# An adaptive-norm, RWKV and mixture-of-experts layer on one core: the shared expert inside the batches' pipeline, and rows that carry base and gate

## What is computed

```python
mod = silu(c) @ wmod                       # per batch: sa, ca, ga, sb, cb, gb (ga, gb kept at least 0.25 in size)
h = layernorm(x) * (1 + ca) + sa
h = ln(h) * g1 + b1
xm = mix(h)                                # this token, the one before, and half of the one before or after
k, v, r = exp(min(xm @ Wk.T, 60)), xm @ Wv.T, xm @ Wr.T
h = h + (sigmoid(r) * wkv(k, v)) @ Wo.T    # two scans over the tokens, and a division
h = ln(h) * g2 + b2
xm = mix2(h)
h = h + sigmoid(xm @ Fr.T) * (relu(xm @ Fk.T)**2 @ Fv.T)      # Fk is 512 x 128
x = x + ga * h
h = layernorm(x) * (1 + cb) + sb
e = argmax(h @ w_router.T)                 # one of 16 experts per token, s = sigmoid(its logit)
routed = (silu(s*h @ G_e) * (s*h @ U_e)) @ D_e                # 256 wide
shared = (silu(h @ w_gate.T) * (h @ w_up.T)) @ w_down.T       # 256 wide
out = x + gb * (shared + routed)
```

## Time and profile before

| | |
|---|---|
| median of three runs | 391.36 us |
| the profiled execution | 393.6 us |
| its span | 391.8 us |
| PE busy | 296.8 us (76%) |
| DVE busy | 244.0 us (62%) |
| ACT busy | 179.3 us (46%) |
| POOL busy | 187.6 us (48%) |
| mean granted PE clock | 0.858 |

### The profile page before, as it was taken

How to read it: one execution, slowest core, us unless ns; L and a number is a source line. 1 busy time by engine, 2 the same in 40 slices (tenths; PEclk the granted TensorE clock), 3 DMA queues, 4 the chain that set the end, 5 groups by cost and what they waited for, 6 DMA issues and landing times.

```text
span 391.8 us, 4364 instructions
## 1 busy us (share of the span) xinstructions
PE 296.8 (76%) x1140; PEld 171.7 (44%) x1140; DVE 244.0 (62%) x514; ACT 179.3 (46%) x436; POOL 187.6 (48%) x267
## 2 busy tenths in 40 slices
PE   4363667877668766877795586699989999999844
PEld 4223234334433534544453343334436666666532
DVE  5148596997989889789688342634335444444423
ACT  2541654947556666555372543222214444444300
POOL 4542726558678485656273534310003666666610
PEclk9956598996998888767889598699999999999955
DMA  6688000102011010010010100132002222222057
GB/s 182 175 241 321 28 0 4 51 0 60 22 47 35 0 54 29 0 41 21 0 49 8 41 14 14 50 97 49 0 1 56 75 75 82 71 77 71 4 155 274
DMA packets 28184, 25.22 MB, mean 64 GB/s; under 512 B 3682, under 2 KB 21734, under 8 KB 28160
## 3 DMA queue, kind: packets, MB, share of 16 engines
q1 hardware_dynamic: 24480, 18.57, 16.5%
q0 software_dynamic: 2528, 4.27, 3.4%
q10 hardware_dynamic: 1152, 2.10, 1.4%
HBM read 17.42 MB, written 8.49 MB: 66 GB/s over the span
## 4 chain that ended last, share of the span: by engine, by line
PE 30%; DVE 24%; POOL 21%; issue 13%; ACT 7%; DMA 3%; SPq 0%; POOLq 0%; DVEq 0%; ACTq 0%
PE bank L858 23%; POOL y_rows L423 11%; PE bank L862 5%; DVE work L524 4%; POOL sorted_rows L400 4%; POOL work L377 3%; ACT work L724 2%; DMA work<-y_rows 2%; DVE work L543 2%; DVE work L519 2%; DVE work L517 1%; DVE work L541 1%; PE bank L901 1%; POOL work L381 1%; DVE work L528 1%
## 5 line engine op out<-in xcount | busy, mean ns | idle before, releaser
L423 POOL DMA_INDIRECT y_rows<-work x47 | 46.2, 982 | 71.2 <-ACT work L838 41.9
L862 PE MATMUL bank<-ident,work 128*128 128x128 f32 x192 | 40.2, 362 | 52.9 <-ACT work L724 23.9
L862 PEld LDWEIGHTS bank<-ident,work 128*128 128x128 f32 x192 | 29.9, 185 | 75.0 <-ACT work L724 28.9
L858 PE MATMUL bank<-up_experts,work 128*128 x94 | 48.2, 595 | 0.0
L685 DVE COPY work<-bank 128x256 f32<-128x256 f32 x47 | 19.9, 424 | 37.7 <-PE bank L1043 37.7
L400 POOL DMA_INDIRECT sorted_rows<-rows,slot_i x32 | 36.5, 1140 | 14.4 <-issue 8.9
L858 PE MATMUL bank<-work,Fk 128*128 128x512 f32 x64 | 34.9, 652 | 5.7 <-DVE work L506 5.7
L724 ACT ACTIVATE work<-work 128x128 f32<-128x128 f32 x64 | 26.3, 487 | 23.5 <-POOL work L381 23.5
L375 POOL TENSOR_SCALAR work<-work 128x4 f32<-128x4 f32 x32 | 6.7, 210 | 59.5 <-DVE work L432 58.6
L377 POOL TENSOR_TENSOR work<-work,neghalf 128x4 f32<-128x4 f32 x32 | 33.2, 1038 | 2.7
L858 PE MATMUL bank<-work,Fv 128*128 128x512 f32 x64 | 33.3, 648 | 0.0
(11 more groups left out here) (161 smaller groups left out, 630.4 us busy)
## 6 DMA issues: line engine op xcount, KB each, us to landing
up_experts<-in_gate_up SPq DMA_DIRECT2D x2, 2048.0 KB, 11.7
work<-sorted_rows SPq DMA_DIRECT2D x47, 66.0 KB, 1.8
work<-in_x SPq DMA_DIRECT2D x8, 256.0 KB, 3.4
work<-in_xT SPq DMA_DIRECT2D x8, 256.0 KB, 3.1
work<-y_rows SPq DMA_DIRECT2D x8, 256.0 KB, 4.2
out_t<-work ACTq DMA_DIRECT2D x8, 256.0 KB, 3.9
sorted_rows<-pad_row SPq DMA_DIRECT2D x17, 66.0 KB, 1.6
y_rows<-work POOLq DMA_INDIRECT x47
```

The source lines that it names most:

```text
L423: pool.indirect_dma_start(y_rows, bass.IndirectOffsetOnAxis(number[q], 0), yb[q], None, bounds_check=NB * T - 1, oob_is_err=False).then_in ...
L858: return pe.matmul(out, w, x, start=start, stop=stop)
L862: last = pe.transpose(out[:, j * P:(j + 1) * P], src[:, j * P:(j + 1) * P], ident[:])
```

## The change

- The shared expert becomes part of each batch's chain in the batch stage. Its down weights are scaled by the gate gb beforehand, per batch (`Wd_gb`, on POOL), and its down product gives token by channel tiles.
- The batch stage's loops run over NB + 12 slots. The chain is cut into single operations, each with a signal of its own, and each engine has a new order. Most buffers between them exist twice. PSUM banks are shared between operations, with a wait for the reader that a bank had before. Silu now comes between Exp and Tanh on ACT. `wkv`'s last product moves from DVE to POOL.
- A row is 386 numbers instead of 132: token, base (x plus gb times shared), gate gb, token number, score. SP fills the gate part by a DMA inside SBUF (`load_gb`). The score is applied inside the expert block: as a scale of the Silu and in DVE's product.
- The expert stage forms the final output rows (product with the gate, plus base, on DVE) and scatters them to the output itself. The copy of the turned activation moves from DVE to ACT. y_rows, its loads, the turns, and the stores at the end are gone. The output has spare rows behind it, into which padding rows go, each with a number of its own.
- SP writes 31 tiles of spare rows to DRAM at the start: 128 x 31 x 384 numbers and 128 x 31 pairs of numbers. The 16 padding tiles after the table are copied from there, DRAM to DRAM.
- The expert weights are loaded in SP's slot 5. The gates' rows are made by eight more products at the start.
- The host no longer turns the output.

The core of the diff:

```diff
-    ROW = C + 4
+    NUM = 3 * C
+    ROW = NUM + 2
-    LAG = 3
+    SPARE = NBLK - NTT
+    LAST = 12
     DEPTH = 6
...
+            def load_gb(b):
+                if b >= 2:
+                    sp.wait_ge(B_out[b % 2].sem, B_out[b % 2].after(b // 2 - 1))
+                sp.dma_start(rows[:, span(b % 2, NT), 2 * C:3 * C], gb_rows[:, b:b + 1, :].broadcast_to([P, NT, C])).then_inc(L_gb[b % 2].sem, 16)
...
+            sp.wait_ge(K_gb.sem, K_gb.after(0))
+            load_gb(0)
+            load_gb(1)
             sp.wait_ge(K_pool.sem, K_pool.after(0))
-            sp.dma_start(sorted_rows[PADS:PADS + P, :], pad_row[:]).then_inc(L_pads.sem, 16)
+            pads = sorted_rows[PADS:, :].rearrange("(k p) r -> p k r", p=P)
+            sp.dma_start(pads[:, :, 0:NUM], pad_row[:].rearrange("p (o r) -> p o r", o=1).broadcast_to([P, SPARE + E, NUM])).then_inc(L_pads.sem, 16)
+            sp.dma_start(pads[:, :, NUM:], pad_id[:]).then_inc(L_pads.sem, 16)
+            for s in range(NB + LAST):
+                if s >= 1 and batch(s - 1 ) and s - 1 >= 2:
+                    load_x(s - 1)
+                if batch(s - 6) and s - 6 >= 2:
+                    load_xT(s - 6)
+                if batch(s - 10) and s - 10 >= 2:
+                    load_gb(s - 10)
+                if s == 1 + 4:
...
+                    sp.dma_start(down_experts[:, 0], ins["down"][:, 0:P, :].rearrange("e p c -> p e c")).then_inc(L_experts.sem, 16)
...
-                sp.dma_start(sorted_rows[bass.ds(at_row, P), :], pad_row[:]).then_inc(L_pads.sem, 16)
+                sp.dma_start(sorted_rows[bass.ds(at_row, P), :], sorted_rows[PADS + (SPARE + e) * P:PADS + (SPARE + e + 1) * P, :]).then_inc(L_pads.sem, 16)
...
-                if i:
-                    sp.wait_ge(D_act.sem, D_act.after(j - DEPTH))
+                if j >= DEPTH:
+                    sp.wait_ge(D_y.sem, D_y.after(j - DEPTH))
...
+            for s in range(NB + LAST):          # DVE
+                if batch(s - 10):
+                    shared_act(0, s - 10)
+                if batch(s - 5):
+                    numerator(s - 5)
+                if batch(s - 6):
+                    norm3_stats(s - 6)
+                if batch(s - 5):
+                    scan_keys(s - 5)
+                    denominator(s - 5)
+                if batch(s - 4):
+                    mix1_before(s - 4)
+                if batch(s - 10):
+                    slots(s - 10)
+                    score(s - 10)
+                if batch(s - 4):
+                    mix1_after(s - 4)
+                if batch(s - 8):
+                    residual2(s - 8)
+                    residual3(s - 8)
+                if batch(s - 3):
+                    norm2_stats(s - 3)
+                if batch(s - 10):
+                    shared_base(s - 10)
+                if batch(s - 5):
+                    gated(s - 5)
+                if batch(s - 4):
+                    clamp_k(s - 4)
+                if batch(s - 5):
+                    invert(s - 5)
+                if batch(s - 8):
+                    norm4_stats(s - 8)
+                if batch(s - 6):
+                    mix2_before(s - 6)
+                if batch(s):
+                    norm1_stats(s)
...
+                if batch(s - 4):
+                    key_value(s - 4)
+                if batch(s - 9):
+                    top_logit(s - 9)
+                    chosen(s - 9)
+                    seen_so_far(s - 9)
+                if batch(s - 7):
+                    residual1(s - 7)
+                if batch(s - 4):
+                    scan_values(s - 4)
+                if batch(s - 9):
+                    shared_act(1, s - 9)
...
             def expert_act(j):
                 q = j % DEPTH
+                dve.wait_ge(D_sg.sem, D_sg.after(j))
+                dve.scalar_tensor_tensor(acte[j % 2], bank[2 + j % 2][:, F:2 * F], xb[q][:, NUM + 1:NUM + 2], sge[j % 2],
+                                         ALU.mult, ALU.mult).then_inc(D_act.sem, 1)
+            def expert_y(j):
...
+                dve.tensor_copy(number[q], xb[q][:, NUM:NUM + 1].bitcast(I32)).then_inc(D_y.sem, 1)
+                dve.wait_ge(D_dn.sem, D_dn.after(j))
+                dve.tensor_tensor(yb[q], bank[6 + j % 2][:, 0:C], xb[q][:, 2 * C:3 * C], ALU.mult).then_inc(D_y.sem, 1)
+                dve.wait_ge(D_y.sem, D_y.after(j, 2))
+                dve.tensor_tensor(yb[q], yb[q], xb[q][:, C:2 * C], ALU.add).then_inc(D_y.sem, 1)
...
+            def project(b):                     # PE: Wo, as one example of the waits
+                pe.wait_ge(A_y.sem, A_y.after(b))
+                pe.wait_ge(A_x1a.sem, A_x1a.after(b))
+                if batch(b + 1):
+                    pe.wait_ge(A_tanh.sem, A_tanh.after(b + 1))
```

More of the change, by code:

```diff
@@ L598, in _ @@
-            dve.wait_ge(B_const.sem, B_const.after(0))
-            for s in range(NB + LAG):
-                if batch(s) and s:
+                if b >= 2:
+                    dve.wait_ge(A_rank.sem, A_rank.after(b - 2))
+                dve.tensor_tensor(by_tile(cand[:]), by_tile(bank[bLG][:, 0:NT * E]), over(top[:]), ALU.is_equal).then_inc(A_hot.sem, 1)
+                dve.wait_ge(A_hot.sem, A_hot.after(b, 1))
+                dve.tensor_tensor(cand[:], cand[:], iota_e[:], ALU.mult).then_inc(A_hot.sem, 1)
@@ L727, in x1, with norm2_rows @@
+            def norm2_rows(b):
+                act.wait_ge(A_sh2.sem, A_sh2.after(b))
+                for j in range(NT):
+                    act.activation(flat(ht[b % 2])[:, span(j, C)], flat(ht[b % 2])[:, span(j, C)], ACT.Identity,
+                                   bias=shift[1][b % 2][:, j:j + 1], scale=rstd[1][b % 2][:, j:j + 1]).then_inc(A_n2.sem, 1)
             def x1(b):
                 act.wait_ge(A_t1.sem, A_t1.after(b))
[L729 to L730 removed]
@@ new lines, in tanh_r2, with norm4_rows @@
+                act.activation(er2, bank[bFR][:], ACT.Tanh, scale=0.5).then_inc(A_tanh2.sem, 1)
+            def keep_x3(b):
+                act.wait_ge(A_st4.sem, A_st4.after(b))
+                if b >= 2:
+                    act.wait_ge(B_out[b % 2].sem, B_out[b % 2].after(b // 2 - 1))
+                act.copy(rows[:, span(b % 2, NT)][:, :, C:2 * C], tok(bT3)).then_inc(A_keep.sem, 1)
+            def norm4_rows(b):
+                act.wait_ge(A_sh4.sem, A_sh4.after(b))
+                if b >= 1:
+                    act.wait_ge(A_t4.sem, A_t4.after(b - 1))
+                for j in range(NT):
+                    act.activation(n4t[:, span(j, C)], bank[bT3][:, span(j, C)], ACT.Identity,
+                                   bias=shift[3][b % 2][:, j:j + 1], scale=rstd[3][b % 2][:, j:j + 1]).then_inc(A_n4.sem, 1)
@@ new lines, in tanh_top, with token_rows @@
+            def tanh_top(b):
+                act.wait_ge(A_top.sem, A_top.after(b))
+                if b >= 1:
+                    act.wait_ge(A_esc.sem, A_esc.after(b - 1))
+                act.activation(etop[:], top[:], ACT.Tanh, scale=0.5).then_inc(A_etop.sem, 1)
+            def token_rows(b):
+                act.wait_ge(A_back.sem, A_back.after(b))
+                if b >= 2:
+                    act.wait_ge(B_out[b % 2].sem, B_out[b % 2].after(b // 2 - 1))
+                act.copy(rows[:, span(b % 2, NT)][:, :, 0:C], tok(bRT)).then_inc(A_rows.sem, 1)
```

1296 lines of the change are left out of this document (768 added, 528 removed).

## The result

The changed kernel takes 402.6 us (median of four runs, 400.7 to 405.8) against 391.1 us for the kernel before, measured beside it (four runs, 390.9 to 398.4): a ratio of 1.031, with a 95% interval of 1.022 to 1.039. It is slower by 3%, and 402.6 lies outside the range of 340 to 397. Every ratio in this document compares only executions in the faster of the two states in which a kernel is seen, so it is not exactly the quotient of the medians beside it. The profiled execution has a span of 399.9 us against 391.8.

What follows compares the result with a forecast made beforehand. Batch stage bound by DVE in the middle and the batch's chain at both ends, shared and expert stages by PE, end by DMA. 52 + 216 + 18.6 + 83 + 2 = 371.6 us of span, so 371 us; range 340 to 397.

Steps and rivals of the forecast that it cites:

- The mechanism of the start: Batch stage's start: x of batch 2 queues behind spare rows and their numbers, so it begins at 52 us, otherwise about 24.
- Rival A: Start: x of batch 2 isn't held by the queue, stage starts near 24, kernel takes 343 us; chance 0.15.
- The middle of the stage: Batch stage, full slots: largest engine sum per slot, plus a waiting factor and 5 us of wait for x.
- the factor 1.08: Batch stage, slots 5 to 12 (138.5 us): allowance for waiting between operations, 11 us.
- both ends, 0 and 18, go to the range: Batch stage's first and last slots: no waiting factor added; 0 and 18 us left to the range.
- for 198 KB 2.3, so T = 1.64, just no change: Expert stage: row load lands in 2.3 us, so the block period stays 1.64; 2 us taken for the stage.
- D_y(j) at 2.4: Expert stage: block's output is formed 2.4 us after row_in(j+3), when its row buffer is released.
- Rival B: Expert stage: row loads become the bound, 3.1 us to land, period 1.9, kernel takes 383 us; chance 0.12.
- the end 2 to 3 us after the last scatter: Kernel's end, a sign to look for: execution ends 2 to 3 us after the last scatter.
- 241 GB/s, still under the rate; 0.6 more: Padding tiles after the table: DRAM to DRAM at 0.82 us an issue, 0.6 us more; 18.6 us on the path.
- C: Batch stage's few-batch slots, 3, 4 and 14 to 17: none under 14 us through PSUM-bank waits, 38 more, 409 us; chance 0.2.
- D: ACT's table switches, 16 in the batch stage: each also empties the engine, 13 us more, 384 us; chance 0.08.

Runs made afterwards that it cites:

- k1: Changed kernel with the two spare-row DMAs moved from ahead of SP's loop into its slot 9: 381.5 us, ratio 0.967.
- k6: k1 with the gate load issued ahead of the xT load in each SP slot: 374.0 us, ratio 0.952.
- k9: k6 with the shared expert's four gate and up products each done twice into the same bank: 398.3 us in one execution.
- k2: Changed kernel with eight row buffers instead of six in the expert stage: 391.7 us, ratio 1.003.
- k3: Changed kernel loading only 520 B of each 1544 B row, base and gate from fixed tiles, six buffers held as long: 394.4 us in one execution.
- k4: Changed kernel with the 16 padding tiles issued half by SP and half by ACT: 402.7 us in one execution.
- k10: k6 plus eight row buffers, padding tiles on two queues, expert weights in slot 8 ahead of xT (spare rows stay in slot 9): 352.1 us, ratio 0.904.
- k11: k10 with four 64 KB writes to spare rows behind the last wait, one after another: 354.9 us in one execution.
- k7: k1 with the expert weights in SP's slot 9 and the spare rows in slot 10: 379.4 us in one execution.
- k5: Changed kernel with the shared expert's work cut to 8 of its 512 columns, waits and signals kept: 403.5 us in one execution.

## Why the prediction was wrong

The predicted span was 371.6 us, the measured one 399.9. Five places make up the difference of 28.3: the start -7.1, the batch stage +13.5 (all but 0.9 of it the drain), the table +5.2, the expert periods +11.4, the end +5.3. The start came out 7.1 better than forecast, and without that the miss would be 35.

**The mechanism of the start held.** The queue order was forecast to keep DVE until 52; it was until 44.9, and k1 shows that the order alone is the cause. Rival A, which had the stage start near 24, falls. The sizes were off both ways. From the issue of the spare rows at 18.3 x of batch 2 takes 25.9 us to land, where the forecast had 18.6 + 12 + 2 = 32.6. By the page of k6 the spare rows alone take 21.2 from issue to landing, so less than 5 are left for the numbers and x together, and 0.05 us for a piece of 8 B was too high a price. No run shows that price by itself.

**The middle of the stage held.** Slots 5 to 11 sum to 121.1 us in the forecast, with the factor 1.08 and the 5 us of wait for x 136; measured 136.4, and the wait is there with 5.01 us. That the sum is so close is in part luck: the slots with the factor and the wait, 18.3, 15.8, 16.5, 18.0, 21.8, 23.1 and 22.2, against the intervals 19.0, 17.0, 18.3, 20.0, 22.7, 20.9 and 18.5, are up to 2 us too short in the first five and 2.2 and 3.7 too long in the last two.

**The first step that failed: "both ends, 0 and 18, go to the range".** In the sum, the slots behind the last reciprocal are 16.1, 12.2, 8, 7.7 and 5, with about 8 of slot 12: 57 us. PE's own work makes up nearly all of that (by the offsets 16.1, 12.2, 7.9, 7.5 and 2.2), and it is nearly exact: 57.8 busy in k6. I took the drain to be this work with no loss, though a factor stood on the slots in the middle. Measured are 69.6. k6, without the gate load's waits, has 62.3 with PE busy for 93% of it: even so 5.3 more than the forecast, and k9 shows that PE's work is the path there. The other 7.3 go with the gate load (k6 has the spare rows later too): its two waits are 5.6 us in the changed kernel, and PE is busy for 59.7 us instead of 57.8, as its clock falls behind the longer one. I had counted the gate load among SP's items only at the start; in the loop it was a move with no price, queued behind an xT load that waits for a reader.

**The second: "for 198 KB 2.3, so T = 1.64, just no change".** The formula was right in kind: k2 takes two more buffers and the period is 1.64 again, k3 takes the size away and most of it goes. And the load was right: the page of k6 gives 2.4 us to landing, in the columns KB of one and median us.

```profile
work<-sorted_rows SPq DMA_DIRECT2D x47, 193.0 KB, 2.4
```

What was wrong in the main is "D_y(j) at 2.4". One turn of a buffer in k6, PE's rows j+3, j+5 and j+6, DVE's last operation on block j, and SP's load into its buffer:

```profile
326.35 0.33 PE L1415 MATMUL bank<-ident,work 128*128 128x128 f32 x1 [0.23 <-DMA work<-sorted_rows]
329.83 0.27 PE L1415 MATMUL bank<-ident,work 128*128 128x128 f32 x1
331.83 0.33 PE L1415 MATMUL bank<-ident,work 128*128 128x128 f32 x1 [0.20 <-DMA work<-sorted_rows]
328.89 0.29 DVE L857 TENSOR_TENSOR work<-work 128x128 f32<-128x128 f32 x1
329.35 0.33 SPq L376 DMA_DIRECT2D work<-sorted_rows  x1
```

From 326.35 the block is finished at 329.18, 2.83 us instead of 2.4; SP issues 0.17 later; the row is there 2.48 after that: 5.48 = 3 x 1.83. The longer hold isn't a result of PE's waits alone, for in k2, where PE has none, the same stretch is 2.74 to 2.80 us in every block. With that the sum is 5.40, and the formula with its 4.9 stood just at three periods of 1.64, so 0.5 us more was all it took. One period in ten or so of the changed kernel lasts 2.35 to 3.35 us, which helps to make 1.889 in the mean; what holds those is open. Rival B, at 383, is this outcome by another route, with T = 1.9 from a load of 3.1 us; it was given 0.12 and came on top of the other faults. I weighed the rivals as if only one of them would happen, while nothing in them excluded the others.

**The third: "the end 2 to 3 us after the last scatter".** In the kernel before the last scatter is followed by 16.9 us of loads and stores, so nothing in its trace shows what a scatter at the end costs. From its start to the end it is 7.7 us, 2.4 of them the landing, and the other 5.3 are the miss. A bound from both sides was missing here.

**The fourth: the pads.** "241 GB/s, still under the rate; 0.6 more" kept 0.82 us a tile. They are issued 1.08 us apart, 17.2 us for 16, and k4 shows the DMA engines full once the issue is halved: 301 GB/s. These DRAM to DRAM copies move less than the 327 GB/s that I had taken from the earlier trace rows. The issue is 4.1 us longer than before, of which 0.6 was forecast; from the last issue to the first load pass 3.1 us instead of 1.8, and that load takes 0.4 more. That is the 5.2.

**Rivals C and D.** C, short slots of at least 14 us: the stage took 23.4 us to the first reciprocal, which is slots 3, 4 and most of 5, near the forecast; at the end two slots were 19 and 21 and the next ones 9.7 and 15.4. It would have given 38 us more; a third of that came, from another cause. PE's work led there (k9), not a wait for a PSUM bank. D, the table switch: six loads of 1.28 us in the whole execution instead of sixteen in the stage. Only the switch between Silu (L1013) and Exp (L924) needs one: at 147.4, 167.0, 171.0, 189.2 and 191.6, the last slots in which both still occur. Tanh and square follow Silu (L964 at 199.5 and 220.3, L970 at 209.0) without a load, and the five Silu slots behind the last Exp are free of them. The Trainium skill ("ScalarE: Activation LUTs", What ACT_TABLE_LOAD costs) adds a drain of 1.38 us to each switch. The idle time in front of the five later loads and behind them is 0.0 to 0.1 us here, and the measurement decides against it.

**The verdict.** What the change takes away was right: 58.2 us of stages. What it puts in their place cost 66, of which 21 lie in one pair of DMAs in the wrong place in a queue, 7 in the gate load's place, and 11 in two missing buffers. k10, which repairs those and leaves the shared expert's place, the order of the engines and the rows as they are, runs in 352 us.

## What to carry to other kernels

Before a change is priced by its engines' work, walk each queue in its issue order and write beside every DMA what stands behind it: 6 MB that nobody needs for 250 us cost 21 us here only by where they stood. Price a wait of TensorE at more than its length when the clock falls behind it, as in k1. A buffer that is held longer and loaded slower needs more copies; set (hold + load) against copies times period, and where the sum comes out just at the period, take the change as slower. And when several independent mishaps are each unlikely, add them: the range has to hold two of them together.

## What the runs showed of the hardware

- A scatter as the last DMA of a program: 7.7 us from its start to the end, of which 2.4 are its landing; with 6.8 us of other transfers behind it the end came only 1.4 us later (k11).
- 3,968 pieces of 8 B in one DMA keep the issuing engine for 11 to 13.7 us (11.02 in the changed kernel, 12.5 in k1 and k10, 13.67 in k7).
- DRAM to DRAM copies of 193 KB: one per 1.08 us from one queue, up to 301 GB/s from two.
- Taking columns out of PE's products can cost what it saves: in k5's one execution the granted clock fell to a mean of 0.61 in a window where the full work had kept it at 1.00.
- Behind a wait of 3.66 us for a DMA in k1 the granted clock was 0.50 for some 6 us; over that drain the same products took PE 64.1 us, and 57.8 in k6, where the wait is gone and the clock 1.00.
- 193 KB in 128 pieces of 1544 B land in 2.4 to 2.5 us with a 64 KB scatter beside each, 66 KB in 1.8.
